# A two-layer graph network on one core: fix-up loop without its carry, a ring of ten quads, and attention values divided in one go

## What is computed

```python
# layer 0: attention over the edges that arrive at a node
xm = x @ W_n2m;  q, k, v = xm @ W_q + b_q, xm @ W_k + b_k, xm @ W_v + b_v   # 4 heads of 16
ee = (edge_attr @ W_edge) @ W_e
alpha = segment_softmax(sum(q[dst] * (k[src] + ee)) / 4, dst)
out = segment_sum((v[src] + ee) * alpha, dst)
x_r = xm @ W_skip + b_skip
beta = sigmoid(concat[out, x_r, out - x_r] @ W_beta)
h = layernorm(x + (beta * x_r + (1 - beta) * out) @ W_m2n)
# layer 1
agg = segment_sum((h @ w2)[src] * edge_weight, dst)
z = layernorm(h + relu(h @ w1 + agg + b))
```

## Time and profile before

| | us |
|---|---|
| median of 3 runs | 1562.85 (1562.12 to 1571.67) |
| span of the profiled execution | 1705.3 |
| stage A, from 61 | 580 |
| end of A and the bridge, 641 to 715 | 74 |
| stage B, 715 to 1056 | 341 |
| turn to stage D, 1056 to 1068 | 12 |
| stage D, 1068 to 1391 | 323 |
| stage C, 1391 to 1697 | 306 |

### The profile page before, as it was taken

One profiled execution on the slowest core, in us unless ns is written; L12 is line 12 of the kernel. 1 busy time (PEld: TensorE's weight loads), 2 busy tenths in 40 slices (PEclk: granted clock), 3 DMA queues, 4 the chain that ended last, 5 costly groups with the idle time before them and its releaser, 6 DMA issues.

```text
span 1705.3 us, 34722 instructions
## 1 busy us (share of the span) xinstructions
PE 1245.0 (73%) x9184; PEld 1095.8 (64%) x9184; DVE 1346.5 (79%) x5156; ACT 1225.0 (72%) x4231; POOL 1042.2 (61%) x1182
## 2 busy tenths in 40 slices
PE   1888888888888882288877876788888876665661
PEld 1877777777777772177766766666666675554551
DVE  2777898889999998888877876799999984654653
ACT  0899999999999995077787876899999962222221
POOL 2666666555566660055555656888888846666665
PEclk9999999999999996599999997999999997787876
DMA  6899999999999996734444445899999942222221
GB/s 189 269 306 302 305 305 304 303 302 301 305 301 305 308 300 233 240 117 152 154 144 140 156 141 168 270 289 292 293 289 294 292 143 77 79 82 74 86 77 38
DMA packets 210148, 372.00 MB, mean 218 GB/s; under 512 B 36740, under 2 KB 67821, under 8 KB 208935
## 3 DMA queue, kind: packets, MB, share of 16 engines
q1 hardware_dynamic: 120822, 200.48, 37.2%
q10 hardware_dynamic: 57771, 108.12, 17.3%
q0 software_dynamic: 31360, 61.17, 13.2%
HBM read 231.39 MB, written 161.37 MB: 230 GB/s over the span
## 4 chain that ended last, share of the span: by engine, by line
ACT 36%; DVE 29%; issue 11%; another core or an unknown queue 9%; PE 9%; DMA 1%; POOL 1%; SPq 1%; DVEq 1%; ACTq 0%; POOLq 0%
ACT hout L728 10%; ACT scan_buf L728 10%; DVE stats L992 7%; DVE hpre L1238 6%; ACT big L756 4%; ACT em L688 3%; DVE big L1228 3%; DVE hpre L1314 2%; ACT lv L769 2%; PE pd L596 2%; DVE hout L1002 2%; DVE scan_buf L1002 2%; PE pd L597 2%; PE pk L619 2%
## 5 line engine op out<-in xcount | busy, mean ns | idle before, releaser
L992 DVE BATCH_NORM_STATS2 stats<-hpre 128x6 f32<-128x256 f32 x882 | 334.8, 421 | 1.8
L466 POOL DMA_INDIRECT ring_a<-in_x,gidx x196 | 185.6, 947 | 207.4 <-PE pt L556 146.7
L728 ACT ACTIVATE scan_buf<-hpre,nb,rs 128x128 f32<-128x128 f32 x686 | 292.1, 480 | 2.8 <-DVE scan_buf L1002 1.3
L728 ACT ACTIVATE hout<-hpre,nb,rs 128x128 f32<-128x128 f32 x686 | 292.2, 480 | 2.5 <-issue 1.2
L1098 DVE SCALAR_TENSOR_TENSOR hpre<-pd,beta,xg 128x128 f32<-128x128 f32 x784 | 221.3, 345 | 29.0 <-DVE beta L1091 1.0
L565 PE MATMUL pd<-w_sx,scan_buf 128*128 128x129 f32 x1568 | 229.7, 276 | 0.0
L469 POOL DMA_INDIRECT ring_b<-in_x,gidx x196 | 185.0, 944 | 60.0 <-issue 60.0
L619 PEld LDWEIGHTS pk<-w_sb,scan_buf 128*128 128x128 f32 x1568 | 211.5, 196 | 7.4
L499 POOL DMA_INDIRECT big<-h_tab,gidx x196 | 193.4, 987 | 35.0 <-POOL big L505 29.5
L619 PE MATMUL pk<-w_sb,scan_buf 128*128 128x128 f32 x1568 | 209.9, 278 | 0.0
L565 PEld LDWEIGHTS pd<-w_sx,scan_buf 128*128 128x128 f32 x1568 | 207.0, 192 | 2.7
(11 more groups left out here) (208 smaller groups left out, 3692.4 us busy)
## 6 DMA issues: line engine op xcount, KB each, us to landing
xg<-in_x SPq DMA_DIRECT2D x196, 256.0 KB
scan_buf<-in_xT SPq DMA_DIRECT2D x196, 256.0 KB
val<-h_tab SPq DMA_DIRECT2D x139, 256.0 KB
h_tab<-hout ACTq DMA_DIRECT2D x98, 256.0 KB
h_tab<-scan_buf ACTq DMA_DIRECT2D x98, 256.0 KB
out_z<-hout ACTq DMA_DIRECT2D x98, 256.0 KB
out_z<-scan_buf ACTq DMA_DIRECT2D x98, 256.0 KB
h_two<-h_tab SPq DMA_DIRECT2D x57, 256.0 KB, 9.1
```

Source lines behind the costliest of these rows:

```text
L466: gp.indirect_dma_start(out=ring_a[:, u, :], out_offset=None, in_=x[:, :], in_offset=bass.IndirectOffsetOnAxis(ap=gidx[:, k, 0:1], axis=0))\
L728: ins = act.activation(hout[ju][:, i * D:(i + 1) * D], hpre[:, ju, i * D:(i + 1) * D], ACT.Identity, bias=nb_of(ju, i), scale=rs_of(ju, i))
L992: ins = dve.bn_stats(stats[:, ju, i, :, :].rearrange("p j s -> p (j s)"), two)
```

## The change

It has two parts.

**Attention values.** After the reciprocal, the factor `cexp` of the carry is multiplied by it (one instruction on DVE) and `val` itself is multiplied by it, head by head, in place: heads 0 and 1 on DVE, heads 2 and 3 on POOL, each one instruction over 128x3136 numbers. The 64 instructions of line 1174 follow, the ones of heads 2 and 3 once POOL is done. `b1_gather_o` is gone: PE turns the columns straight from `val` (64 numbers at a stride of 196), in two transposes instead of one, and ACT evicts 64 partitions by 256 columns instead of 128 by 128.

**Fix-up.** The carried runs are left out of stage C's loop: their scatter index is pushed past the bound, and one extra row on each partition is computed after the loop. The four `carg` instructions of a quad and the wait behind them are gone, so relu reads PSUM directly. The output ring is ten quads in `val` instead of four buffers. The multiplication by the edge weight moves from POOL in stage D to ACT, and the run sums from stage D to two quads ahead of their use in stage C, but for the first eight columns. The sums are also stored to `agg_scr`, from which the extra rows are gathered.

```diff
+            gp.wait_ge(S["sc"], 6)
+            for h in range(HD, H):
+                over_sum(gp, h).then_inc(S["scaled"], 1)
...
-            for k in range(T + GL):
-                if k < T:
-                    if k >= UG:
-                        gp.wait_ge(S["agg_b2"], k - UG + 1)
-                    gp.indirect_dma_start(out=agg[:, k, :], out_offset=None, in_=h_tab[:, :],
...
-                    gp.tensor_tensor(agg[:, j, :], agg[:, j, :], ew_t[:, j:j + 1].to_broadcast([P, D]),
-                                     ALU.mult).then_inc(S["agg_b2"], 1)
+            for k in range(T):
+                if k >= UG:
+                    gp.wait_ge(hs_in[k % UG], 16 * (k // UG))
+                gp.indirect_dma_start(out=agg[:, k, :], out_offset=None, in_=h_tab[:, :],
...
+            for q in range(T4 - 4):
+                scatter_quad(q)
+            gp.wait_ge(S["agg_st"], 16 * T4)
+            gp.indirect_dma_start(out=agg_x, out_offset=None, in_=agg_scr[:, :],
...
+            gp.indirect_dma_start(out=h_x, out_offset=None, in_=h_tab[:, :],
...
+            for q in range(T4 - 4, T4):
+                scatter_quad(q)
+            gp.wait_ge(S["sc"], 11)
+            gp.indirect_dma_start(out=out[:, :],
+                                  out_offset=bass.IndirectOffsetOnAxis(ap=rows_x[:, 1:2], axis=0),
...
             def b1_turn(k):
-                pe.wait_ge(S["os_b1"], k + 1)
                 if k > 0:
                     pe.wait_ge(S["oT_b1"], k)
-                pe.transpose(pt[:, 1, 0:P], o3[:, k % 2, :], ident[:, :]).then_inc(S["t_b1"], 1)
+                for i in range(2):
+                    mm = pe.transpose(pt[0:DM, 1, i * P:(i + 1) * P], o_rows[:, :, 2 * k + i], ident[:, :])
+                mm.then_inc(S["t_b1"], 1)
...
-                    if j > 1:
-                        pe.wait_ge(S["cy_c"], j - 1)
+                    if j > 1:
+                        pe.wait_ge(S["u_c"], j - 1)
...
+            def weigh_rows(t):
+                act.wait_ge(hs_in[t % UG], 16 * (t // UG + 1))
+                act.activation(agg[:, t, :], agg[:, t, :], ACT.Copy, scale=ew_t[:, t:t + 1]).then_inc(S["agg_b2"], 1)
...
+            for k in range(T4 + 1):
+                if k < T4:
+                    if 2 <= k:
+                        c_evict(k)
+                    for t in range(NJ * (k + KQ), min(NJ * (k + KQ + 1), T)):
+                        weigh_rows(t)
+                if k > 0:
+                    j = k - 1
                     inv_std(act, stats[:, j % U, :, :, 2], 1.0 / D, lv[:, j % U, :, :], rs[:, j % U, :, :],
                             S["bn_c"], S["lv_c"], S["rs_c"], j)
...
+            dve.reciprocal(alpha[:, :, :], alpha[:, :, :]).then_inc(S["sc"], 1)
+            dve.wait_ge(S["sc"], 6)
+            link(dve.tensor_tensor(cexp[:, :, :], cexp[:, :, :], alpha[:, :, :], ALU.mult))
             for h in range(H):
+                if h < HD:
+                    link(over_sum(dve, h))
+                else:
+                    dve.wait_ge(S["scaled"], h - HD + 1)
                 for c in range(C):
...
             for k in range(T4 + 1):
                 if k < T4:
                     dve.wait_ge(S["mm_c"], k + 1)
...
-                    for i in range(NJ):
-                        t = NJ * k + i
-                        ins = dve.scalar_tensor_tensor(out=hpre[:, ku, i * D:(i + 1) * D], in0=carg,
-                                                       scalar=psame[:, t:t + 1], in1=pk[:, k % 2, i * D:(i + 1) * D],
-                                                       op0=ALU.mult, op1=ALU.add)
-                    ins.then_inc(S["cy_c"], 1)
+                    dve.scalar_tensor_tensor(out=hpre[:, ku, :], in0=pk[:, k % 2, :], scalar=0.0, in1=xg[:, ku, :],
+                                             op0=ALU.max, op1=ALU.add).then_inc(S["u_c"], 1)
+                    for t in range(NJ * (k + KQ), min(NJ * (k + KQ + 1), T)):
+                        run_sum(t)
                     dve.wait_ge(S["u_c"], k + 1)
                     pair_stats(ku, NJ // 2).then_inc(S["bn_c"], 1)
+                if k > 0:
+                    g = k - 1
+                    dve.wait_ge(S["rs_c"], g + 1)
+                    if g >= UZ:
+                        dve.wait_ge(z_sc[g % UZ], NJ * 16 * (g // UZ))
+                    normalise(lambda i: z_rows(g)[:, i * D:(i + 1) * D],
+                              lambda i: hpre[:, g % U, i * D:(i + 1) * D], g % U, NJ).then_inc(S["z_c"], 1)
```

More of the change, by code:

```diff
@@ L27 @@
 NP = 1
+PADDED, FILLS, FILL_E, DROPS, R_O, DSTEPS, ROWS = range(1, 8)
 QSCALE = 1.0 / C ** 0.5
@@ L84, in gnn_kernel @@
     UV = 12
+    HD = 2
+    UZ = 10
+    KQ = 2
     TC = T // 4
@@ L281, in gnn_kernel, with z_rows @@
         hv_in = [sem(f"hv_in{i}") for i in range(UV)]
+        z_sc = [sem(f"z_sc{i}") for i in range(UZ)]
+        def z_rows(q):
+            i = UV + q % UZ
+            return val_row[:, i * GN:(i + 1) * GN]
         def h_rows(g):
@@ L596, in b1_product @@
                     pe.matmul(o, xdT_all[:, 2 * j + i, :], w_sx[:, :], start=False, stop=False)
-                    mm = pe.matmul(pd_bank[:, j % 2, i, 0:D + 1], oT[j % 3], r_o[:, i, :], start=False, stop=True)
+                    mm = pe.matmul(pd_bank[:, j % 2, i, 0:D + 1], oT(j)[:, i * P:(i + 1) * P], r_o[j % 2 * DM:(j % 2 + 1) * DM, j % 2, :], start=False, stop=True)
                 mm.then_inc(S["mm_b1"], 1)
@@ L636, in _ @@
                 d2_product(g - 1)
-            def carry_turns():
-                pe.wait_ge(S["sc"], 7)
-                pe.transpose(pt[:, 0, 0:P], sum_a, ident[:, :])
-                pe.transpose(pt[:, 0, P:2 * P], sum_b, ident[:, :]).then_inc(S["sc_pe"], 1)
-            def carry_product():
-                pe.wait_ge(S["sc"], 8)
-                pe.matmul(pt[:, 1, 0:D], cumT[:, 0:P], w2_sb[:, :], start=True, stop=True).then_inc(S["sc_pe"], 1)
             for k in range(T4 + 1):
@@ L674, in _ @@
                     mm.then_inc(S["mm_c"], 1)
-                if k == 1:
-                    carry_turns()
+            pe.wait_ge(S["sc"], 8)
+            pe.transpose(pt[:, 0, 0:P], run_a, ident[:, :])
+            pe.transpose(pt[:, 0, P:2 * P], run_b, ident[:, :]).then_inc(S["sc_pe"], 1)
+            pe.wait_ge(S["x_in"], 2 * 16)
+            pe.transpose(pt[:, 1, 0:P], h_x, ident[:, :])
+            pe.transpose(pt[:, 1, P:2 * P], agg_x, ident[:, :]).then_inc(S["sc_pe"], 1)
+            pe.wait_ge(S["sc_act"], 6)
+            pe.wait_ge(S["sc"], 9)
+            pe.wait_ge(S["u_c"], T4)
+            o = pk[:, 0, 0:D]
+            pe.matmul(o, ones3[:, :], bias3[:, 2 * D + 1:3 * D + 1], start=True, stop=False)
+            pe.matmul(o, hT_x, w1_sb[:, :], start=False, stop=False)
+            pe.matmul(o, aggT_x, w2_sb[:, :], start=False, stop=False)
+            pe.matmul(o, run_cumT[:, 0:P], w2_sb[:, :], start=False, stop=True).then_inc(S["sc_pe"], 1)
         def inv_std(act, spread, per, log_v, r, mv_sem, lv_sem, rs_sem, j):
@@ new lines, in _ @@
+                if k == T4 - KQ:
+                    dve.wait_ge(S["run_b2"], T - 1)
+                    dve.tensor_copy(run_a, agg[:, T - 1, :])
+                    dve.tensor_copy(run_b, psame[:, T - 1:T].to_broadcast([P, D])).then_inc(S["sc"], 1)
+            dve.wait_ge(S["sc_pe"], 5)
+            dve.memset(run_cumT[:, 0:1], 0.0)
+            link(dve.tensor_copy(run_keepT, pt[:, 0, P:2 * P]))
+            dve.tensor_tensor_scan(run_cumT[:, 1:P + 1], run_keepT, pt[:, 0, 0:P], 0.0, ALU.mult, ALU.add)\
+                .then_inc(S["sc"], 1)
@@ new lines, in _ @@
+            dve.wait_ge(S["sc_pe"], 7)
+            link(dve.scalar_tensor_tensor(out=u_x, in0=pk[:, 0, 0:D], scalar=0.0, in1=h_x, op0=ALU.max, op1=ALU.add))
+            dve.bn_stats(stats_x[:, :, :].rearrange("p j s -> p (j s)"),
+                         u_x.rearrange("p (f j) -> p f j", j=1).to_broadcast([P, D, 2])).then_inc(S["sc"], 1)
+            dve.wait_ge(S["sc"], 10)
+            dve.wait_ge(S["sc_act"], 8)
+            dve.tensor_scalar(z_x, u_x, stats_x[:, 0, 1:2], rs_x[:, 0:1], ALU.subtract, ALU.mult).then_inc(S["sc"], 1)
```

235 lines of the change are left out of this document (124 added, 111 removed).

## The result

The kernel after takes 1643.95 us in the median (1636.76 to 1656.35 over 4 runs), the kernel before 1562.48 on the same chip (1561.49 to 1571.67 over 4): a ratio of 1.051 with a 95% interval of 1.045 to 1.057, slower by 81 us. The forecast was 1591, with a range to 1622.

The account below looks back on a forecast made before the run. Without late PE signals, DVE and ACT bound stage D, ACT stage B and POOL stage C. Bridge +21, stage B +10, stage D -6 and stage C +3 made +28 on 1562.85: 1591 us, range 1555 to 1622.

Parts of the forecast that it names:

- The base: Whole kernel: 1562.85 us median without late PE signals; stage B bound by ACT at 5.48 us a pair, stage C by POOL.
- the late signals of PE: Stages B and C: profiled waits of 69.7 and 44.7 us on PE, taken as absent or nearly so from timed runs.
- The rival in which the ring covers those signals: Stage C: late PE signals also occur in timed runs, ten quads of output rows cover them, saving 45 us: 1546 us; chance 0.12.
- The bridge, +21: Between reciprocal and stage B: dividing values on DVE and POOL, which take turns, adds 21 us; bounds +7 to +27.
- the 14 us of POOL: Between reciprocal and stage B: POOL's multiplies for two heads, 7 us each, paid on the path because DVE is blocked.
- The rival without blocking: Between reciprocal and stage B: DVE and POOL work side by side, so this part costs 7 us; total 1577 us; chance 0.22.
- Stage B, +10: Stage B: ACT sets the pace, its wider eviction adds 0.10 us a step over 98 steps; PE hidden; bounds 0 to +15.
- the rival of the gains in B and D: Stages B and D gain more than seen, DVE having been B's pace: 1571 us; chance 0.06.
- Stage D, -6: Stage D: without run sums and POOL multiplies in DVE's way, ACT sets 2.065 us a group: 6 us saved; bounds -9 to +3.
- Stage C, +3: Stage C: POOL stays the bound at 5.3 us a quad over a 5.05 us loop; extra gathers and scatter; bounds -2 to +8.
- The prediction's own sign of being wrong: Stage C: the forecast is wrong if POOL waits for DVE outside stops, or never waits there at all.
- The rival of the loop: Stage C: relu, run sums, turns and product at 1.2 GHz for a third of quads, 7.7 us each; +20, 1611 us; chance 0.18.

Follow-up runs that it names:

- own buffers: Kernel after with a 128-row buffer for each stage B step's transposed rows, the product reading all 128 rows against zero-padded weights: 1604.2 us, ratio 1.025.
- three ahead: Run sums three quads ahead instead of two in stage C: kernel after so edited 1606.01 us (1.027); the fix-up part alone so edited 1553.49 us (0.993).

## Why the prediction was wrong

The sign was right, the size was not: +28 forecast, +81 measured, 22 us beyond the range.

*The base.* That the late signals of PE did not belong to the timed runs was right. What I took from between them, 5.48 us a pair, was 0.22 short of the 5.70 of an undisturbed execution. The rival in which the ring covers those signals fell with them.

*The bridge, +21.* Measured +21.2 in length. The mechanism is shown from both sides (9.89 against 3.41 us, and 6 us less without POOL). Inside the sum the 14 us of POOL were 13.2 of its own work, of which 12.9 landed on DVE. The rival without blocking is refuted. The Trainium skill's "SBUF — State Buffer", section "Who interferes with whom", is borne out by it for the long instructions that no row of before had.

*Stage B, +10: the step that failed.* It counted one transpose more a step and ACT's longer copy, and said "So I count PE as hidden". It never costed the product itself, whose weights and rows go from 128 to 64 partitions: a term put at nothing without a reason. That costs 0.28 us a half, makes PE the bound at 6.34 us a pair, and is 32.5 us. The copy, which was the whole term, cost nothing; nor did the stage gain anything from the 98 gathers that DVE lost (own buffers: 5.70 us a pair, as before), so the rival of the gains in B and D is refuted too.

*Stage D, -6.* Measured -7.2.

*Stage C, +3: the second step that failed.* The loop was found and sized (5.05 us; measured 5.06). Wrong was the comparison: 5.05 was set under POOL's 5.3 with PE at full clock, because "most of that is the stops" was to explain the clock of 0.78. Executions without a single stop have 0.83 before and 0.78 after. And POOL's pace proved 5.2 us a quad (254.8 us for 195 distances between scatters with three ahead), so the margin was smaller still. The prediction's own sign of being wrong came: POOL waits for DVE inside the stage, 134.6 - 76.8 = 57.8 us in 40 waits. The rival of the loop named the mechanism and gave it 20 us for a third of the quads; it was 30 of 48, at 6.7 us and not 7.7, and 45 us in the profile. A margin of 0.25 us between a loop that holds idle PE time and a bound is none. With the loop broken the stage is 4 us shorter than before's, where I had said 3 longer; these 4 us lie behind the last transfer, and up to POOL's last issue the two are alike, 275.4 and 275.6 us.

## What to carry to other kernels

Before narrowing a matmul's contraction to fewer partitions than its neighbours have, look at where its weight load starts; here the loads that no longer lay under other matmuls cost more than the zero rows they saved, and padding with zeros was free. When an edit reorders work into a loop across engines, compare the loop at half TensorE clock, not at full, with what bounds the stage, for every loop in which PE waits, and give the producer one more step of lead. Splitting a two-input elementwise pass between DVE and POOL was no split: they took turns, and DVE alone was 6 us faster.

## What the runs showed of the hardware

A load of 128-row fp32 weights started 0.22 us ahead of its own matmuls, under 128-row matmuls; a 64-row load in the same place waited 0.33 us and started with its matmuls, and the 128-row load behind the 64-row matmuls (863.05) started with its own as well. The 64-row load's length is the same, 0.186 us against 0.190. The Trainium skill, "TensorE: Matmul & The Clock Gate", section "The mechanism", says that a weight load overlaps matmuls in flight only where the row groups differ, though it also names the background weight buffer as a place that a load may go to ahead of them. By the rule on row groups both loads would have waited, since the matmuls ahead of them use all 128 rows; the traces show it for the 64-row load alone, and they decide.

Twelve products of 256 columns a quad, which nobody reads, took 40 us off the kernel, by keeping the granted clock at 1.00 from 1325 to 1575 (0.96 over the whole stage) where the stage had 0.78. The same page's section "HAM oscillation — how this bites in real kernels" describes a PE that idles between bursts and starts each new one cold; the rows of stage C agree in part, with 1.97 us of PE's idle time a quad ahead of the turns of agg in after, and 0.73 (34.3 us over 47 waits) in the run where the needless products fill it; but after's quads at full clock had the 1.97 us too. How much work it takes to hold the clock wasn't tried.
